# Rank 1 of a MoE row scatter with two indirect DMAs in flight in place of one

## What is computed

```python
gate = jnp.einsum('bsd,ed->bse', x, Wg) + routing_bias
_, top_idx = jax.lax.top_k(gate, K)                    # K = 4 of E = 8
weights = probs * mask                                 # softmax over the chosen
out = _swiglu(x, Ws1, Ws2, Ws3)                        # the shared expert
h1 = jnp.einsum('bsd,ehd->ebsh', x, W1)
h2 = jnp.einsum('bsd,ehd->ebsh', x, W2)
eo = jnp.einsum('ebsh,edh->ebsd', jax.nn.sigmoid(h1) * h1 * h2, W3)
out = out + jnp.einsum('ebsd,bse->bsd', eo, weights)
```

## Time and profile before

| | |
|---|---|
| time, median of 3 runs | 1042.13 us (1039.98 to 1045.28) |
| time of the profiled execution | 1038.96 us |
| its span | 1035.8 us |
| PE busy | 988.5 us, 95% |
| POOL busy | 531.6 us, 51% |
| DVE busy | 590.0 us, 57% |
| rank 0, rank 1, rank 2, rank 3 on POOL | from 134.5, 202.1, 307.7, 405.5 us |
| expert 0, 1, 2, 3 on PE | from 213.8, 345.7, 475.0, 526.2 us |

### The profile page before, as it was taken

The page is one execution under the profiler, slowest core; times in us unless marked ns, Lnnn a source line. Parts: engine busy times, 40 slices in busy tenths (PEclk is TensorE's granted clock), DMA queues, the critical chain, the costliest instruction groups (busy, mean ns, idle before and its releaser), DMA issues.

```text
span 1035.8 us, 27298 instructions
## 1 busy us (share of the span) xinstructions
PE 988.5 (95%) x8630; PEld 840.9 (81%) x8630; DVE 590.0 (57%) x1680; ACT 525.4 (51%) x1367; POOL 531.6 (51%) x501
## 2 busy tenths in 40 slices
PE   9997989979999999999999999999999999999986
PEld 4556867867888888888878888888888888887875
DVE  3998896545545454544545445545455454444786
ACT  3675644434555455545545554545454554554465
POOL 3554054358233234843648007066888861884870
PEclk9997999989999999999999999999999999999999
DMA  8946132443532333253243423228864872885792
GB/s 249 224 114 167 22 84 85 141 92 84 176 97 83 95 98 103 83 174 99 69 145 84 108 48 101 70 54 173 127 98 78 127 111 52 122 123 85 95 163 92
DMA packets 167891, 113.83 MB, mean 110 GB/s; under 512 B 113436, under 2 KB 160031, under 8 KB 166688
## 3 DMA queue, kind: packets, MB, share of 16 engines
q0 software_dynamic: 30480, 59.41, 27.0%
q1 hardware_dynamic: 114960, 32.07, 15.4%
q10 hardware_dynamic: 22400, 21.76, 6.1%
HBM read 47.09 MB, written 40.96 MB: 85 GB/s over the span
## 4 chain that ended last, share of the span: by engine, by line
PE 43%; DMA 28%; POOL 12%; issue 7%; DVE 6%; ACT 1%; SPq 0%; ACTq 0%; POOLq 0%; DVEq 0%
PE psA L996 28%; DMA rows_by_place<-y_rows,place 25%; PE psB L1023 10%; POOL y_sum L702 4%; POOL rows_by_place L658 3%; POOL work L588 2%; PE psA L947 1%; POOL work L581 1%; POOL stage L582 1%; DMA y_sum<-rows_by_place,place 1%; PE psC L978 1%; PE psB L1026 1%; DVE g_lo L1406 1%; DMA rows_by_place<-zeros,pad_at 1%; DVE work L1202 1%
## 5 line engine op out<-in xcount | busy, mean ns | idle before, releaser
L816 ACT ACTIVATE sil<-psA 128x256 f32<-128x256 f32 (+1 forms) x510 | 187.1, 373 | 289.0 <-PE psA L996 214.9
L1396 DVE SCALAR_TENSOR_TENSOR g<-psA,sil 128x256 f32<-128x256 f32 (+1 forms) x178 | 73.5, 414 | 315.3 <-ACT sil L816 288.2
L658 POOL DMA_INDIRECT rows_by_place<-y_rows,place x128 | 127.5, 996 | 225.7 <-DMA rows_by_place<-y_rows,place 178.3
L702 POOL DMA_INDIRECT y_sum<-rows_by_place,place x128 | 198.6, 1552 | 84.6 <-DMA rows_by_place<-eb 39.3
L996 PE MATMUL psA<-xb_odd,work 128*128 128x256 f16 x2112 | 235.8, 273 | 1.8 <-issue 1.2
L996 PE MATMUL psA<-xb,work 128*128 128x256 f16 x2046 | 230.7, 274 | 6.9 <-issue 4.5
L996 PEld LDWEIGHTS psA<-xb_odd,work 128*128 128x128 f16 x2112 | 206.1, 98 | 26.9 <-issue 3.2
L996 PEld LDWEIGHTS psA<-xb,work 128*128 128x128 f16 x2046 | 200.6, 98 | 33.1 <-issue 9.0
L1023 PE MATMUL psB<-work,g_hi 128*128 128x256 f16 x1320 | 221.1, 273 | 4.1 <-DVE g_lo L1406 3.6
L1396 DVE SCALAR_TENSOR_TENSOR psC<-psA,sil 128x256 f32<-128x256 f32 (+1 forms) x332 | 140.1, 422 | 82.4 <-ACT sil L816 69.6
L1023 PE MATMUL psB<-work,g_lo 128*128 128x256 f16 x660 | 179.9, 273 | 0.0
(11 more groups left out here) (159 smaller groups left out, 842.0 us busy)
## 6 DMA issues: line engine op xcount, KB each, us to landing
stage<-wpack POOLq DMA_DIRECT2D x9, 2176.0 KB, 9.1
rows_by_place<-eb ACTq DMA_DIRECT2D x63, 256.0 KB
work<-half_beta SPq DMA_DIRECT2D x8, 512.0 KB, 4.9
work<-x_tok POOLq DMA_DIRECT2D x8, 512.0 KB, 6.0
work<-xT SPq DMA_DIRECT2D x7, 512.0 KB, 4.5
rows_by_place<-y_rows,place POOLq DMA_INDIRECT x128, 2.5
y_sum<-rows_by_place,place POOLq DMA_INDIRECT x128
out<-y_sum ACTq DMA_DIRECT2D x4, 512.0 KB
```

Of the source, the lines that this page charges most:

```text
L658: pool.indirect_dma_start(out=xs, out_offset=bass.IndirectOffsetOnAxis(ap=place[:, k, n:n + 1], axis=0), in_=y_rows[:, n, :], in_offset=No ...
L702: pool.indirect_dma_start(out=y_sum[:, n, :], out_offset=None, in_=xs, in_offset=bass.IndirectOffsetOnAxis(ap=place[:, k, n:n + 1], axis=0 ...
L816: act.activation(sil[r0:r0 + n, c % SLOTS, 0:T], psA[0:n, c % HVS, 0:T], ACT.Silu, scale=1.0 / (XS * WS)).then_inc(silu_ready, 1)
L1396: dve.scalar_tensor_tensor(gated_rows(g, c, 0, n, T), src, 1.0 / (XS * WS), sil[r0:r0 + n, c % SLOTS, 0:T], ALU.mult, ALU.mult).then_inc(g ...
```

## The change

Rank 1 is called with `overlapped` = NT, so that each of its 32 scatters waits for the one before the last, through the semaphore of its own parity. Ranks 0, 2 and 3 keep their waits. Nothing else changes, and no engine's instructions stand in another order.

```diff
             pool.wait_ge(blocks_ready, 1)
             pool.wait_ge(pads_written[0], 16)
-            scatter(1, 0, convert_beside(1, 5, 20))
+            scatter(1, NT, convert_beside(1, 5, 20))
             pad_rows(1)
             pool.wait_ge(pads_written[1], 16)
             scatter(2)
```

## The result

| | before | after |
|---|---|---|
| time, median | 1043.7 us (1039.98 to 1047.2, 4 runs) | 1033.06 us (1031.54 to 1033.99, 4 runs) |
| time of the profiled execution | 1038.96 us | 1033.75 us |
| its span | 1035.8 us | 1032.0 us |
| rank 1 on POOL, first scatter to padding | 202.1 to 304.4 us | 200.6 to 277.4 us |
| expert 0's first up product on PE | 213.8 us | 211.9 us |

The ratio is 0.9895, with an interval from 0.985 to 0.994: faster by 1%. The forecast of 1040.5 us and the range from 1036 to 1046 are both missed, on the low side.

What follows compares the result with a forecast made beforehand. It took PE, not the scatters, to bound: 3.3 us gained from fewer conversion delays in rank 1, 1.7 lost in rank 3, other terms 0, so -1.6 us from the 1042.13 median gives 1040.5 us, range 1036 to 1046.

Runs made afterwards that it cites:

- e3: Kernel before with ranks 1, 2 and 3 all at two scatters in flight: 1084.56 us, ratio 1.0373.
- e11: Kernel before with rank 2 at two scatters in flight and expert 2's weight fetch moved behind rank 1's scatter 31: 1067.11 us, ratio 1.0243.
- e5: Kernel before with rank 1 at two in flight up to scatter 16, then pairs that each wait for the pair before: 1035.32 us, ratio 0.9951.
- e12: Kernel before with rank 1 two in flight to scatter 16, then pairs, and expert 3's conversion behind rank 3's scatters 20 to 31: 1036.66 us, ratio 0.9942.
- e15: Kernel before with expert 2's weight fetch behind rank 1's scatter 31 and rank 2's scatters in pairs: 1034.25 us, ratio 0.9938.
- e17: Kernel before with ranks 1 and 2 in pairs, expert 1's conversion and expert 2's fetch behind rank 1's padding: 1035.75 us, ratio 0.995.
- e9: The changed kernel unedited, measured a third time against the kernel before: 1039.4 us, ratio 0.9988.
- e2: The changed kernel unedited, measured again beside the kernel before on one chip: 1042.85 us, ratio 0.9975.

## What to carry to other kernels

Where the chain of waits runs for a quarter of the span through an engine that ends in a small wait of the bounding engine, the two may be level: size that wait by what it becomes when the bounding engine has a good execution, not by the one row, and get a second profile of the unchanged kernel first. That the DMA engines have room doesn't make more DMAs in flight free beside a busy TensorE: look for blocks in which matmuls come in fives with idle time "issue" between them, and leave a gap after each pair.

## What was not expected of the hardware

- Held blocks: 16.6 to 37.2 us in place of 10.7, PE beginning one to five matmuls every 0.72 or 1.43 us with no semaphore named, ACT idle for 8.45 us beside it, at DMA shares of 0.35 and 0.37; it ended within 3 us of the padding behind the run of scatters each time. It begins at the full clock; in e3 and e11, where it goes on, the clock falls to 0.50. It was seen with rows of 1056 bytes only, never with rows of 32 bytes.
- Two scatters in flight go 1.27 and 1.45 us apart, one in flight 2.7. With pairs no block was held in e5, e12, e15 or e17.
- The start of expert 0 varies by 6.5 us between the profiles of this study, 210.9 to 217.5 us, and by 6.2 between two of the changed kernel (e9, e2), whose first scatters of rank 0 lie as far apart, at 134.7 and 141.0.
- After an idle time of 5.15 us the next block took 13.14 us in place of 10.70, at a granted clock of 0.50 in its first 4 us. The first block of expert 0, after 4.1 to 4.4 us idle, has the same low clock, for some 3 to 6 us, and its up part varies by it from 8.6 to 10.1 us.
